# A decoder's last layers on one core: all four chains of layers first, then the eight tiles, and gathers that begin at the last chunk's indices

## What is computed

```
x = x + L3_attn(layernorm(x))     # 4 inner layers: retention with a decaying state along the tokens, then an FFN with gelu
x = x + L3_xattn(ctx, ctx, layernorm(x), mask)
      # K, V = projections of the context; q = h @ Wq + bq
      # off = q @ Woff + boff            -> 5 positions per token and head (16 heads): 80 per token
      # loc = mod(base + off, length - 1); i0 = floor(...), i1 = i0 + 1
      # sk = 0.5*(w0*K[i0] + w1*K[i1]), sv likewise; softmax over the 5; sum; output projection
x = x + L3_ffn(layernorm(x))      # 8 experts relu(h @ W1 + b1) @ W2 + b2; each token takes 2 of them, by a hash of its row
```

## Time and profile before

| | us |
|---|---|
| median of 3 runs | 6831.65 |
| lowest, highest run | 6809.26, 6833.71 |
| the profiled execution's own time | 6840.76 |
| its span in the trace | 6838.9 |
| of that, from the start of chain 0 to the end | 1748.4 |

### The profile page before, as it was taken

One profiled execution on the slowest core, in us unless ns is written; L12 is line 12 of the kernel. 1 busy time (PEld: TensorE's weight loads), 2 busy tenths in 40 slices (PEclk: granted clock), 3 DMA queues, 4 the chain that ended last, 5 costly groups with the idle time before them and its releaser, 6 DMA issues. The chain is left out here.

```text
span 6838.9 us, 85925 instructions
## 1 busy us (share of the span) xinstructions
PE 4632.7 (68%) x32744; PEld 1821.5 (27%) x32744; DVE 3726.1 (54%) x8316; ACT 2693.4 (39%) x4917; POOL 753.7 (11%) x949
## 2 busy tenths in 40 slices
PE   5856999514899999998638999997855050424326
PEld 1222444312122222222421222221343030323315
DVE  5454666456777777772349898992244040412314
ACT  1321666232566666664016787874101010101103
POOL 0100000001000000000010000000001707062350
PEclk9567999756999999999668999996975555555557
DMA  0020000042000000000030100000040000000000
GB/s 12 0 56 8 14 10 9 13 173 73 1 11 11 11 11 11 11 1 6 0 94 1 21 11 11 11 11 12 0 147 2 13 2 13 2 11 5 6 10 3
DMA packets 105757, 142.14 MB, mean 21 GB/s; under 512 B 41982, under 2 KB 82013, under 8 KB 102496
## 3 DMA queue, kind: packets, MB, share of 16 engines
q1 hardware_dynamic: 65694, 117.88, 6.6%
q0 software_dynamic: 20480, 10.53, 1.0%
q10 hardware_dynamic: 19178, 8.34, 0.5%
HBM read 103.53 MB, written 33.14 MB: 20 GB/s over the span
## 5 line engine op out<-in xcount | busy, mean ns | idle before, releaser
L1812 ACT ACTIVATE probs<-ps 128x512 f32<-128x512 f32 x3264 | 1734.2, 598 | 794.4 <-PE ps L1757 794.2
L1847 DVE CUSTOM_DVE_ANT_0 junk<-ps,mask 128x512 bf16<-128x512 f32 (+1 forms) x1664 | 1049.1, 678 | 383.2 <-PE ps L1719 367.1
L1842 DVE TENSOR_REDUCE maxima<-ps 128x2 f32<-128x1024 f32 (+1 forms) x832 | 956.2, 1199 | 127.5 <-PE ps L1719 121.1
L1773 PE MATMUL ps<-probs,vstack 128*9 128x512 f32 x6528 | 894.4, 610 | 0.2 <-ACT probs L1812 0.2
L1757 PE MATMUL ps<-qturned,kturned 52*128 52x512 bf16 x3264 | 808.7, 392 | 78.2 <-ACT probs L1812 59.3
L1719 PE MATMUL ps<-kturned,qturned 49*128 49x512 bf16 (+1 forms) x3328 | 704.3, 392 | 142.3 <-DMA kturned<-ends_row 59.2
L3122 POOL DMA_INDIRECT line<-table,index x640 | 609.9, 953 | 1268.1 <-DVE index L3393 646.2
L1750 PE MATMUL ps<-maskT,lower 128*128 128x512 fp8e5 x1632 | 562.5, 387 | 63.5 <-ACT probs L1812 15.1
L1757 PEld LDWEIGHTS ps<-qturned,kturned 52*128 52x128 bf16 x3264 | 195.0, 93 | 818.3 <-ACT probs L1812 489.2
L1719 PEld LDWEIGHTS ps<-kturned,qturned 49*128 49x128 bf16 x3328 | 166.2, 95 | 523.7 <-issue 236.3
L3446 DVE SCALAR_TENSOR_TENSOR x_sb<-ps,gate,x_sb 128x128 f32<-128x128 f32 x64 | 22.4, 351 | 498.8 <-DMA rows<-in_ctx 321.1
(11 more groups left out here) (730 smaller groups left out, 5619.1 us busy)
## 6 DMA issues: line engine op xcount, KB each, us to landing
raw<-in_mask_BxSxS_if SPq DMA_DIRECT2D x8, 3202.0 KB, 13.2
kturned<-keys_parts SPq DMA_DIRECT2D x192, 102.0 KB
table<-lines SPq DMA_DIRECT2D x51, 256.0 KB, 2.8
line<-table,index POOLq DMA_INDIRECT x640
keys_parts<-parts SPq DMA_DIRECT2D x24, 384.0 KB, 2.5
values_heads<-vall SPq DMA_DIRECT2D x2, 3672.0 KB, 10.7
vstack<-values_heads SPq DMA_DIRECT2D x16, 459.0 KB, 16.7
lose<-in_mask_SxS_bc SPq DMA_DIRECT2D x32, 128.0 KB
```

The costliest lines, as they stand in the source:

```text
L1773: last = nc.tensor.matmul(k.ps[at:at + HD + 1, 3, :], vstack[:, p % 2, a, t, :], probs[:, (h * KT + t) % slots, a, :], start=(t < 2), stop ...
L1812: nc.scalar.activation(probs[:, u % slots, a, :], k.ps[:, (2 * u + a) % 3, :], ACT.Exp, scale=(1.0 if maskT is None else 1.0 / STEP8)).the ...
L1842: nc.vector.tensor_reduce(dst, ring(e).rearrange("p (a n) -> p a n", a=2)[:, :, 0:hi - lo], AX.X, ALU.max).then_inc(ring_free[at % 2], 1)
L1847: nc.vector.tensor_tensor_reduce(junk[:, at % 2, a * BANK:a * BANK + hi - lo], ring(e)[:, a * BANK:a * BANK + hi - lo], mask8[:, 4 * b + m ...
```

## The change

`last_steps` returns the four chains first and then the eight posts. GpSimd waits once, ahead of its first gather, for the indices of the last chunk, in place of a wait at each chunk; its waits for `used` of tile t - 4 stay. No instruction that computes is added or taken away.

```diff
@@ last_steps
-    steps = [("chain", c) for c in range(CHUNKS_OF_T - 1)] + [("post", t) for t in range(CHUNK)]
-    return steps + [("chain", CHUNKS_OF_T - 1)] + [("post", t) for t in range(CHUNK, NT)]
+    return [("chain", c) for c in range(CHUNKS_OF_T)] + [("post", t) for t in range(NT)]
@@ last_layer, block.gpsimd
+            pool.wait_ge(vector_done, by_dve("index", CHUNKS_OF_T - 1))
             for t in range(NT):
-                if t % CHUNK == 0:
-                    pool.wait_ge(vector_done, by_dve("index", t // CHUNK))
                 if t >= 4:
                     pool.wait_ge(vector_done, by_dve("used", t - 4))
                 for j in range(HN):
```

## The result

| | kernel before | changed kernel |
|---|---|---|
| median | 6820.45 us (4 runs, 6800.32 to 6833.71) | 6886.93 us (4 runs, 6880.19 to 6892.98) |
| ratio, 95% interval | | 1.010 (1.0068 to 1.0131) |
| span of the profiled execution | 6838.9 | 6891.1 |
| what comes before chain 0 | 5090.5 | 5060.3 |
| last stage, from chain 0 to the end | 1748.4 | 1830.8 |

A forecast was written before the change was run, and what follows sets the result against it. PE was taken to nearly stand still beside gathers' packets, an unnamed wait. Terms -339.1 + 112.9 + 268.0 + 1.3 = +43.1 us on 6831.65 gave 6874.8 us, range 6852 to 6908.

The forecast's parts named there:

- the 0.5% bound: Whole kernel: what a measurement can tell from no change, about 0.5% or 34 us, 6865.8 us.
- Chains: Last stage, chains 1 to 3 at 180.9 us each without gathers: 542.7 us for 881.8, -339.1 us.
- The wait for tile 0: Before the first post: PE, ACT and DVE wait for the first tile's gathers, +112.9 us.
- Post 0: First post, beside four tiles' gathers, PE at 2.80 us a matmul: 402.5 us for 134.5, +268.0 us.
- rival B: First post: an idle PE is granted a burst again, 82 us less there; +32 in all, 6864 us; 12%.
- Post 1: Second post: one tile's gathers beside it, begun from an idle queue, so 133.2 us as before.
- C: Row of 400 gathers: a long row is worse, gathers say 1.5 us apart, +103 and 6935 us; 8%.
- Posts 2 and 3: Third and fourth posts: one tile's gathers beside each, as before, at the mean of 133.2 us.
- Posts 4 to 7 with the store: Last four posts: no gather left, 152.8 us to the end of the span, as before.
- Rival A: Last stage: gathers don't slow PE, so GpSimd bounds it; -171.0 us, 6660.6 us; 5%.

The follow-up runs named there:

- the version with short rows: Changed kernel's step order, with GpSimd gathering eight lines at two marks per layer in chains 1 to 3, the rest without pause: 6636.91 us with hold-up, 6366.87 without.

## Why the prediction was right, and where it wasn't

The direction held, and so did the cause, that a gather holds the work beside it up and is waited for when it has nothing beside it: the time is in the range and beyond the 0.5% bound, on the slower side. That it lies only 12 us above the value is in part luck, since the kernel before came out at 6820.45 and not at 6831.65: the change is +66.5 us, 23 more than forecast. Against the last stage the forecast was low by 39.3 us (1830.8 for 180.9 + 542.7 + 112.9 + 402.5 + 399.7 + 152.8 = 1791.5), and the profiled execution came within 9 us of the 6882.0 forecast for its span only because what lies ahead of the stage was 30.2 us shorter in it. Term by term:

- *Chains*, 542.7 forecast, 542.7 measured. That every chain follows a chain, and not chain 3's 178.6 us, was the right choice. Since nothing but the gathers' place changed for chains 1 and 2, they were the whole cause of the long chains.
- *The wait for tile 0*, 112.9 forecast, 101.5 measured, 11.4 too much. I had said that packets begin 12.4 us behind the first issue and end as much behind the last. The first line of the earlier trace rows speaks against it: in those 12.4 us it has a DMA share of 0.08, as in the stretch behind. The packets go with the issue, and DVE's `near` of tile 0 begins 2.4 us behind the start of its last gather:

```profile
5883.27 0.94 POOL L3120 DMA_INDIRECT line<-table,index  x1 [0.30 <-issue]
...
5885.71 1.49 DVE L3398 TENSOR_TENSOR near<-line,frac 128x1280 f32<-128x1280 f32 x1 [101.36 <-DMA line<-table,index]
```

  What lags is the hold-up, not the packets: in the kernel before it sets in some 16 us after the first gather, and it outlasts the row, by 26 us in the changed kernel, with a DMA share of 0.00.
- *Post 0*, 402.5 forecast, 399.3 measured, but not for the reason given. It was to need 429 us and to be cut short by the end of the row; it needed 399.3 and the row went on. Additions did lie 50.4 us apart (six of seven gaps are 49.7 to 50.4); the first came 69.3 us into the post, where 26 + 26 x 2.80 = 99 was the working. That is a credit of some ten matmuls, rival B in small. Nor is PE alone in standing still, as the prediction has it: DVE got one instruction in 1.40 us too, which cost nothing because PE took longer.
- *Post 1*, 133.2 forecast, 185.3 measured: the term that was mis-sized, 52.1 us. Two things that I had given to rivals came together. The gathers slowed to 1.40 us apart from the 210th on (C), so the row of tiles 0 to 4 ended later; and post 0 was over by then (B), so tile 5's gathers followed without a gap, 480 in a row, and post 1 ran beside them from its beginning. The step that failed is the sentence that takes a post with a gather "begun from an idle queue". B's sum did not see the slower gathers, and C's had nothing but an example of 1.5 us.
- *Posts 2 and 3*, 266.4 forecast, 266.6 measured. *Posts 4 to 7 with the store*, 152.8 and 154.2.

Rival A had 5%, as the chance that the page's rule holds. With hold-up it fell. Without hold-up it is what happens, and its time was close: 6667.9 - 5090.5 = 1577.4 us of stage forecast, 1573.7 measured. What it could not say is that the kernel before would then be some 700 us faster too, so that the change is not 171 us faster but 530 us slower. I compared a rival's time for the changed kernel with a kernel before that the same rival would have changed. In both conditions the change is slower; the sign was safe, the size was not.

## What to carry to other kernels

A gather that is moved behind the work that covered it is paid for in full (101.5 us for one tile); moving it away from work that it seems to slow pays only what the hold-up was costing, and that can differ from one set of runs to the next. Where a trace shows a long unnamed wait, put the kernel before into each set of runs and look at its time first: every experiment here would have been misread without it. And a rival on the hardware has to be worked out for both kernels, not for the changed one alone.

## What the runs showed of the hardware

- Two conditions, with the same kernels. With hold-up, PE beside a row of gathers gets one instruction in 1.40 us (50.4 us for 36, 72.8 us for 52), and so does DVE, at the same time: in post 0 of the changed kernel DVE goes at that pace from 5901.70 to 5931.11, while PE's eight matmuls and eight weight loads for the relu of expert 1 take 22.4 us (relu at 5904.50 and 5926.90), 16 times 1.40. Each instruction of DVE and ACT keeps its own duration (0.15 us, and 1.14 us for four of relu); what is held up is its start. From some 190 to 210 gathers in a row on, gathers come 1.40 us apart too, in place of 1.25. Without hold-up, PE did 148 matmuls beside 80 gathers in the 37.6 us that they need (101.6 less the 64.0 us of waiting), and 144 gathers cost a chain nothing. One chip showed both conditions, in different sets of runs, so it does not go with the chip alone. It isn't the granted clock either: 0.54 beside gathers in a chain of 181.5 us, 0.52 in one of 352.2. What sets it stays open; no run here could switch it. Two rivals stand untested. That the pace is per instruction, on two engines at once, would fit instructions that arrive late as well as an engine that can't start them. And every run on record was traced (each comes with its span and granted clock), so none shows whether the tracing takes part.
- The hold-up has a credit and a tail. It sets in some 16 us into a row that begins with the work, and eight gathers with pauses of 6 to 16 us never reach it. But the row's age alone doesn't decide: in posts 0 and 1 of the changed kernel, 101 and 500 us into a row, DVE had waited, and its first 24 or 25 instructions went at full pace. The tail grows with the row. From the start of the last gather to the first addition that is no longer held up it took 13 us behind 80 gathers (post 0 of the kernel before, last gather at 6078.00), and 28.5 us behind 216 (the version with short rows, last gather at 6051.96):

```profile
6091.17 0.35 DVE L3446 SCALAR_TENSOR_TENSOR x_sb<-ps,gate,x_sb 128x128 f32<-128x128 f32 x1 [15.13 <-DMA rows<-in_ctx]
...
6080.50 0.35 DVE L3449 SCALAR_TENSOR_TENSOR x_sb<-ps,gate,x_sb 128x128 f32<-128x128 f32 x1 [27.70 <-DMA rows<-in_ctx]
```

  Behind 400 and 480 gathers it is 28.6 and 27.4 us, no longer than behind 216. This looks like something that fills and drains, but no view shows what.
- A gather issued while DVE blends two inputs from on-chip memory takes 2.25 us of POOL in place of 0.94; `near` itself stays at 1.49 us:

```profile
5885.77 2.25 POOL L3120 DMA_INDIRECT line<-table,index  x1 [0.30 <-issue]
```

  With the two gathers behind it, of 1.22 and 1.23 us, that is 1.8 us a tile: 51.7 us in place of 49.9 for 40 gathers. The Trainium skill has this ("SBUF — State Buffer", section "Who interferes with whom": a DVE instruction with two SBUF inputs contends with GpSimd when that reads SBUF), and here the trace agrees.
